# Attention with a top-2 expert layer: a joined prologue, a fourth help tile on VectorE, moved jobs and a last store in two pieces

## The chip, the cores and the metric

One core of one Trainium2 chip runs the whole kernel. The time is that of one execution on the device, in microseconds. Its engines each run their own queue of instructions and meet at semaphores: TensorE (PE) for matmuls and transposes, ScalarE (ACT) for exponentials and copies, VectorE (DVE) for elementwise work, GpSimd (POOL) for indirect transfers and some elementwise work, SyncE (SP) for most transfers.

## What is computed

```python
x: (4, 1024, 128) fp32
xn = layernorm(x)
# attention, 16 heads of 8 channels, rotary positions, on xn
attn = softmax((rope(xn @ Wq.T) . rope(xn @ Wk.T)) * 8**-0.5) . (xn @ Wv.T)
# expert layer on xn: 8 experts, the best 2 of each token, three linear layers
gates = softmax(xn @ gate_w + gate_b); top 2
h = gelu(xn @ w1 + b1); h = gelu(h @ w2 + b2); e = h @ w3 + b3
out = x + attn + sum(top2_gate * e)
```

## The kernel before

**Steps.** Attention is cut into 16 steps (`STEPS`), one for each batch and group of four heads. A step has two halves of 512 queries, and a half has eight blocks (`MT`) of 128 keys: 64 pieces of 128 keys x 512 queries for one head each. For a piece TensorE multiplies keys and queries (the scores, in PSUM), ScalarE takes the exponential into `probs`, and TensorE multiplies it with the values into `o_ps` ("values", one block of four heads at a time). A column of ones in the values gives the sum of the exponentials. After a step VectorE copies `o_ps` (`copy_o`), TensorE transposes the copy (`turn`), and VectorE divides (`normalise`).

**Prologue (L613 to L660, L762 to L858, L1273 to L1320).** The rows of the first batch are normalised (`statistics`, `invert_first`), turned eight in a row with filler matmuls between (L1284, L1287), and projected by `first_projection(g)` (L1300): g = 0 keys and 1 queries of the first 512 rows, 2 and 3 of the second. VectorE multiplies the products with cosine and sine tables (L820, L822); GpSimd or VectorE adds them (L534, L827); ScalarE or GpSimd makes a rounded high part, and the low part is the difference (L541, L829). The parts go from SBUF to `k_st` and `q_st` by transfers (L383, L657) and to DRAM (`store_parts`) for the steps to come. `WARM` (10) and `WARM_AGAIN` (4) filler matmuls run at the start and ahead of the first scores. The scores wait for `k00_loaded` (128 keys), `q0_loaded` and `proj_read` 4.

**Steps 0 and 1** take two heads at a time (1024 columns, L672). **Steps 2 to 8** take three at a time (L694): a half has 11 groups, ten of three heads and the last of two. PSUM holds two groups. The order on TensorE is written out in `step()`: in slot g come the scores of group g + 1, which wait for the exponential of group g - 1; an extra job where `JOB_PLACE` has one (slots 1, 5, 9, 12, 16, 20); and the values of the block that ended in group g - 1. Slots 0, 2, 3, 4, 6, 7, 8 and 10 of a half have values, slots 1, 5 and 9 have none. `plan_jobs()` gives each job its place in sixteenths of a step: `turn` of the step before, `plain` (a projection of a later batch: one matmul of 512 columns, L1343, then `plain_part`, an exchange of rows by SP, and `join_parts` some places later), `values`, `norm`, `count`, `bound`. `ROUTE` spreads the routing arithmetic on VectorE, and `ROUTE_EXP` places its one exponential in ScalarE's queue (L682). All jobs use the one PSUM bank `aux_ps`, and each waits for VectorE's reading of the one before. SP reloads `k_st` and `q_st` half by half; a load for step t waits for the stores of that batch (`stored_before`).

**Experts** (296 to 424 us) run on sorted tokens; the change leaves them alone.

**Steps 9 to 15** (`late_step`) have 20 groups of three (`LATE_ITEMS`): both halves but the first key block of the second half. That block is the help block: four tiles of 128 x 512, whose scores TensorE puts into `aux_ps` one by one in slots 2 to 5 (L1534). VectorE reads the first three (L1192) and makes their exponentials by a polynomial in eight instructions on 128 x 1536 (L1202 to L1210); ScalarE takes the fourth after its eighth group (L733). In slot 17 TensorE waits for both and multiplies them with the values (`help_values`, L1556). Between VectorE's reads stand the additions of expert outputs (`combine`, L1176, six instructions each time), whose rows GpSimd gathers (L610) into the one buffer `gath`. The last step divides its halves apart: `copy_o`, `turn`, `normalise`, `finish_rows` (L1186) and the last store (L502) follow each other.

```python
if HELP_AT <= g < HELP_AT + HG:
    help_scores(t, g - HELP_AT)      # slots 2 to 5
if g == HELP_AT + 7 and not first:
    turn(t - 1, 0, True)             # slot 9
if g == HELP_VALUES:
    help_values(t)                   # slot 17
```

Of the kernel before, what the change touches and what calls it, by code (L numbers as in the profile page):

```python
# [16 lines left out]
F32 = mybir.dt.float32  # L17
# [10 lines left out]
HG = 4  # L28
# [34 lines left out]
WARM = 10  # L63
WARM_AGAIN = 4
WARM_LATE = (3, 1)
FIRST_SCATTER = 66

# [13 lines left out]
def heads_of(g):  # L81

    r = g % HALF_GROUPS
    return [divmod(n, HG) for n in range(3 * r, min(3 * r + 3, MT * HG))]
# [15 lines left out]
LATE_ITEMS = [(0, mt, h) for mt in range(MT) for h in range(HG)] + [(1, mt, h) for mt in range(1, MT) for h in range(HG)]  # L100
LATE_GROUPS = len(LATE_ITEMS) // 3
LATE_BLOCKS = [(0, mt) for mt in range(MT)] + [(1, mt) for mt in range(1, MT)]
HELP_AT = 2
HELP_HEADS = (0, 3, 2, 1)
HELP_VALUES = 17
EXP_COEFFS = (-7.287735462188721, 41.80864715576172, -180.93753051757812, 522.0867309570312, -753.2122192382812)
# [24 lines left out]
TURN_PLACES = (1, MT // 2)  # L131
# [9 lines left out]
def plan_jobs():  # L141

    turns = {BLOCKS * t + TURN_PLACES[t >= GROUPED]: ("turn", t - 1) for t in range(1, SPLIT)}
    fixed = {0: ("values", 0, 2), 7: ("norm", 0), 64: ("norm", 1), 94: ("norm", 2), 126: ("norm", 3), 54: ("count",),
# [8 lines left out]
    for b, places in ((1, (10, 11, 12, 13, 14, 15)), (2, (18, 20, 21, 22, 24, 26)), (3, (27, 28, 30, 31, 32, 34))):  # L153
# [15 lines left out]
ROUTE_EXP = (2, 11)  # L169
ROUTE = {divmod(block, BLOCKS): n for n, block in enumerate((39, 42, 43, 44, 47, 49, 51, 52, 53, 54, 55, 56, 57, 58, 59, 60, 61, 62, 63, 65, 66))}  # L170
# [18 lines left out]
def build(nc, x, Wq, Wk, Wv, w1, b1, w2, b2, w3, b3, gw, gb, rope_cos, rope_sin, consts, out):  # L189
    ctx = ExitStack()  # L190
    with ctx:
# [99 lines left out]
        gath = part(0, 2 * GATHER * C).rearrange("p (k c) -> p k c", c=C)  # L291
        he_s, he_t, he_g, he_p = (part(2 * GATHER * C + 3 * HALF * k, 3 * HALF) for k in range(4))
# [9 lines left out]
        proj_ps = [bank(2, 2), bank(4, 2)]  # L302
# [14 lines left out]
        help_probs = probs[:, PROB_RING - 1]  # L317

        def group_probs(phase, g):
# [7 lines left out]
        names = """x_loaded0 x_loaded0b x_loaded1 x_loaded2 x_loaded3 small_loaded gate_loaded rope_loaded0 rope_loaded1 bias_loaded  # L327
            wT_made wT_copied stats_made std_made rows_made batch_rows_made trans_done xnT0_made proj_done proj_read
            rot_made0 rot_made1 hi_made0 hi_made1 again_made0 again_made1 lo_made0 lo_made1 sq_made0 sq_made1 parts_stored0 parts_stored1 parts_stored2 parts_stored3
            exchanged0 exchanged1 parts_cleared k00_loaded v0_done v0_copied v0_read aux_done aux_read dve_chain dve_pro_chain  # L330
# [5 lines left out]
            gathered combined comb_chain out_ready out_stored  # L336
            fb_loaded fb_v_loaded fb_scores fb_max fb_shift fb_exp fb_turned fb_copied fb_pv fb_chain fb_normed fb_ready fb_stored""".split()
        S = {n: sem(n) for n in names}
        parts_stored, rot_made, hi_made, again_made, lo_made, sq_made, y_stored, xs_in, rope_loaded, exchanged = (
            [S[f"{n}{k}"] for k in range(4 if n in ("parts_stored", "xs_in") else 2)] for n in ("parts_stored", "rot_made", "hi_made", "again_made", "lo_made", "sq_made", "y_stored",  # L340
                                                       "xs_in", "rope_loaded", "exchanged"))
# [5 lines left out]
        def _(sp):  # L347
# [44 lines left out]
            first_load(0, S["k00_loaded"], 0, P)  # L392
            first_load(0, S["ka_loaded"], P, HALF)
# [106 lines left out]
            for n, (tile, tiles) in enumerate([(b * BT, BT) for b in range(B - 1)] + [((B - 1) * BT, BT // 2), (TILES - BT // 2, BT // 2)]):  # L500
# [19 lines left out]
        def _(pool):  # L520
# [83 lines left out]
            for i in range(STEPS - SPLIT - 1):  # L604
                if i >= 1:
                    pool.wait_ge(S["combined"], i)
# [1103 lines left out]
```

## Time and profile before

| | |
|---|---|
| median of 3 runs | 628.67 us (628.52 to 629.24) |
| the profiled execution | 628.49 us, its span 626.7 us |
| busy share of the span | PE 95%, ACT 86%, DVE 54%, POOL 31% |
| chain that ended last | PE 62%, ACT 17%, issue 12%, DVE 5%, DMA 2% |

Times in the rows are microseconds from the start of the span. A matmul's end is modelled, so TensorE's pace is read from start to start. ScalarE's and VectorE's instructions overlap the start of the next a little, and a timeline row joins instructions of one line that follow without a break.

### The profile page before, as it was taken

Reading aid. Unit: us, or ns where it says so; the run is one execution under the profiler, and the core shown is the slowest. Engines: PE = TensorE matmul, PEld = TensorE weight load, DVE = VectorE, ACT = ScalarE, POOL = GpSimd, SP = SyncE. Lnnn points to the kernel's source line nnn. Section 1 sums busy time; section 2 is a strip of 40 time slices with the busy share of each in tenths; the row PEclk is TensorE's granted clock in tenths of the full one; section 3 lists DMA queues with packets and bytes.
Section 4 is the critical chain, followed back from the end, with each engine's and each line's share of the span. In section 5 each row is a group of like instructions: output and inputs, shape, how many; then the busy total and the mean of one; then the engine's idle time right before and its main releaser. Section 6 shows DMA issues by size and latency. Waiting matters only on the chain.

```text
span 626.7 us, 12150 instructions
## 1 busy us (share of the span) xinstructions
PE 595.1 (95%) x4128; PEld 255.9 (41%) x4128; DVE 335.7 (54%) x795; ACT 536.0 (86%) x548; POOL 196.6 (31%) x187
## 2 busy tenths in 40 slices
PE   8889999999999999999999999998999999999996
PEld 6323332232222222232899999983222222222221
DVE  5654322776263335021565555546394958668475
ACT  3799999999999999999455555559999999999995
POOL 2700000000444544441122222223655748484000
PEclk9999999999999999999999999999999999999998
DMA  7653711443264626693433333310312112131311
GB/s 231 171 197 133 264 44 35 162 159 119 85 223 164 219 85 227 205 296 76 99 75 81 71 73 75 75 44 19 110 35 84 59 59 67 55 87 55 116 40 38
DMA packets 82622, 70.69 MB, mean 113 GB/s; under 512 B 44288, under 2 KB 58400, under 8 KB 82576
## 3 DMA queue, kind: packets, MB, share of 16 engines
q1 hardware_dynamic: 76000, 56.34, 29.7%
q0 software_dynamic: 5856, 13.05, 6.8%
q10 hardware_dynamic: 720, 0.71, 0.5%
q8 instruction: 25, 0.41, 0.3%
q14 instruction: 21, 0.17, 0.1%
HBM read 32.92 MB, written 32.96 MB: 105 GB/s over the span
## 4 chain that ended last, share of the span: by engine, by line
PE 62%; ACT 17%; issue 12%; DVE 5%; DMA 2%; ACTq 0%; SPq 0%; DVEq 0%
PE ps L1491 11%; PE ps L1425 10%; ACT probs L729 9%; PE ps L1475 7%; PE ps L1548 6%; ACT probs L694 5%; PE ps L1417 5%; PE ps L1438 5%; PE ps L1521 4%; PE ps L1398 4%; ACT probs L672 2%; PE ps L1343 2%; PE ps L1378 2%; PE ps L1306 1%; DVE x_all L1176 1%
## 5 line engine op out<-in xcount | busy, mean ns | idle before, releaser
L694 ACT ACTIVATE probs<-ps 128x1536 f32<-128x1536 f32 (+1 forms) x154 | 205.2, 1435 | 3.3 <-PE ps L1475 2.9
L729 ACT ACTIVATE probs<-ps 128x1536 f32<-128x1536 f32 x140 | 190.2, 1516 | 2.1 <-PE ps L1521 1.9
L572 POOL DMA_INDIRECT slots_x_d<-xn_all,slot_i x64 | 63.4, 991 | 191.7 <-DVE expert_i L1033 125.0
L1491 PE MATMUL ps<-probs,v_st 128*32 128x512 f32 x896 | 119.3, 605 | 0.6 <-ACT probs L694 0.6
L708 ACT ACTIVATE work<-ps,work 128x256 f32<-128x256 f32 (+1 forms) x156 | 64.9, 455 | 60.4 <-PE ps L1425 60.2
L1548 PE MATMUL ps<-probs,v_st 128*32 128x512 f32 x840 | 111.4, 604 | 0.5 <-DVE o_sb L918 0.5
L610 POOL DMA_INDIRECT work<-slots_y_d,slot_i x64 | 89.8, 1404 | 64.7 <-PE ps L1548 48.5
L1475 PE MATMUL ps<-q_st,k_st 32*128 32x512 f32 x448 | 77.2, 494 | 6.2 <-ACT probs L694 4.5
L1521 PE MATMUL ps<-q_st,k_st 32*128 32x512 f32 x420 | 71.1, 494 | 8.8 <-ACT probs L729 8.7
L1475 PEld LDWEIGHTS ps<-q_st,k_st 32*128 32x128 f32 x448 | 28.9, 181 | 118.9 <-ACT probs L694 91.0
L1521 PEld LDWEIGHTS ps<-q_st,k_st 32*128 32x128 f32 x420 | 26.4, 181 | 108.0 <-ACT probs L729 99.0
L1425 PE MATMUL ps<-work 128*128 128x256 f32 (+1 forms) x312 | 67.9, 361 | 0.0
L672 ACT ACTIVATE probs<-ps 128x1024 f32<-128x1024 f32 x64 | 60.6, 1034 | 3.8 <-PE ps L1378 2.9
L591 POOL DMA_DIRECT2D slots_y_d<-work x39 | 26.7, 685 | 113.3 <-DVE work L1094 108.8
L1425 PEld LDWEIGHTS ps<-work 128*128 128x128 f32 x312 | 53.0, 191 | 5.0
L1208 DVE SCALAR_TENSOR_TENSOR work<-work 128x1536 f32<-128x1536 f32 x28 | 49.2, 1757 | 0.9
L1438 PE MATMUL ps<-work 128*128 128x128 f32 x284 | 38.2, 275 | 0.0
L1438 PEld LDWEIGHTS ps<-work 128*128 128x128 f32 x284 | 37.2, 191 | 1.8 <-issue 0.2
L918 DVE COPY o_sb<-ps 128x512 f32<-128x512 f32 x17 | 11.8, 691 | 47.9 <-PE ps L1548 29.7
L1417 PE MATMUL ps<-work 128*128 128x256 f32 (+1 forms) x156 | 37.2, 361 | 0.0
L1398 PE MATMUL ps<-probs,v_st 128*32 128x512 f32 x256 | 34.1, 604 | 3.0 <-ACT probs L672 2.1
L837 DVE COPY v_st<-v_all 128x128 f32<-128x128 f32 x32 | 8.3, 260 | 41.4 <-PE ps L1491 21.5
(193 smaller groups left out, 552.8 us busy)
## 6 DMA issues: line engine op xcount, KB each, us to landing
k_d<-parts SPq DMA_DIRECT2D x8, 1024.0 KB, 4.6
q_d<-parts SPq DMA_DIRECT2D x8, 1024.0 KB, 5.2
q_st<-q_d SPq DMA_DIRECT2D x30, 256.0 KB, 3.4
k_st<-k_d SPq DMA_DIRECT2D x30, 256.0 KB, 3.0
slots_x_d<-parts SPq DMA_DIRECT2D x5, 1024.0 KB, 7.5
work<-slots_x_d SPq DMA_DIRECT2D x128, 32.0 KB, 1.9
slots_y_d<-work POOLq DMA_DIRECT2D x32, 128.0 KB, 2.2
work<-work SPq DMA_DIRECT2D x24, 128.0 KB, 2.0
```

Of the source, the lines that this page charges most:

```text
L610: nc.gpsimd.indirect_dma_start(out=gath[:, GATHER * c + k, :], out_offset=None, in_=slots_y_d, in_offset=bass.IndirectOffsetOnAxis(ap=slot ...
L672: nc.scalar.activation(probs[:, j % PROB_RING, 2 * pair:2 * pair + 2, :], score_slot(j, pair).rearrange("p (h n) -> p h n", h=2), ACT.Exp, ...
L694: nc.scalar.activation(group_probs(phase, g)[:, 0:size, :], group_slot(g)[:, 0:size * HALF].rearrange("p (h n) -> p h n", n=HALF), ACT.Exp ...
L708: nc.scalar.activation(dst[:, par, k, rows], src[k][:, rows], ACT.Gelu, bias=b12_st[:, par, n, k:k + 1])\
L729: nc.scalar.activation(late_probs(g), group_slot(g).rearrange("p (h n) -> p h n", n=HALF), ACT.Exp, scale=SCALE).then_inc(S["exp_done"], 1)
L1417: nc.tensor.matmul(h1_ps[m][:, 0:units * ST], w1_sb[:, n % 2, m * P:(m + 1) * P], xsT[:, n % 2, 0:units * ST], start=True, stop=True).then ...
L1425: ins = nc.tensor.matmul(h2_ps[m][:, 0:units * ST], w2_sb[:, n % 2, k, m * P:(m + 1) * P], h1[:, n % 2, k, 0:units * ST], start=(k == 0), ...
L1438: ins = nc.tensor.matmul(y_ps[par][:, m, 0:C], h2[:, par, k, m * P:(m + 1) * P], w3_sb[:, par, k, :], start=(k == 0), stop=(k == 1))
L1475: ins = nc.tensor.matmul(group_slot(g)[:, n * HALF:(n + 1) * HALF], k_st[32 * h:32 * h + ROWS, mt * P:(mt + 1) * P], q_st[32 * h:32 * h + ...
L1491: ins = nc.tensor.matmul(o_ps[32 * h:32 * h + 32, :], v_window(mt, h, half), group_probs(phase, half * HALF_GROUPS + g)[:, n, :], start=(j ...
L1521: ins = nc.tensor.matmul(group_slot(g)[:, n * HALF:(n + 1) * HALF], k_st[32 * h:32 * h + ROWS, mt * P:(mt + 1) * P], q_st[32 * h:32 * h + ...
L1548: ins = nc.tensor.matmul(o_ps[32 * h:32 * h + 32, :], v_window(mt, h, half), late_probs(g)[:, k, :], start=begins, stop=ends)
```

## The change

*Prologue.* Identity and weights get their own transfer count (`weights_loaded`); `WARM` is 7, two fillers follow the weights' transposes, the fillers between the row transposes and `WARM_AGAIN` go. The variance is made with fewer small operations (the root takes a scale of 0.25). The order is: first four rows turned, queries projected (g = 1), the first 256 keys' products, the other rows turned, the other keys, g = 2, one value tile group, g = 3. The first 256 keys are rotated, split and loaded apart (`k00_*`). VectorE takes one copy of values and the high parts of g = 2. The first scores wait for `proj_read` 3; block 1's scores are issued ahead of the wait for the value reads.

*Steps 2 to 8.* `first_of` makes the tenth group of a half the one of two heads (27, 28), and the eleventh has three (29, 30, 31); in the last half of step 8 it stays as before. Jobs get new places: `turn` goes to place 6 (slot 9), in step 2 to place 14; `plain` jobs move to places 0, 8 and 12; each join is four or more blocks after its job; the routing pieces follow; the routing exponential goes ahead of group 14 instead of 11. SP waits for the query store only ahead of the query load.

*Steps 9 to 14.* The help block is the first key block of the first half, and VectorE takes all four tiles: its instructions are 128 x 2048 wide. ScalarE has no help exponential. `combine` comes after `normalise`; `gath` has two buffers. In step 15 the help is as before (three tiles and one), and its combine comes after the polynomial.

*End.* The last half is copied in two pieces and turned two tiles at a time, its early columns are summed and stored ahead, and the last sum and store have 32 of the 128 columns.

```diff
-WARM = 10
-WARM_AGAIN = 4
+WARM = 7
+WARM_ROWS = 2
+START_KEYS = 2 * P
+def first_of(r, ending=False):
+    return min(3 * r - (r == HALF_GROUPS - 1 and not ending), MT * HG)
-    return [divmod(n, HG) for n in range(3 * r, min(3 * r + 3, MT * HG))]
+    return [divmod(n, HG) for n in range(first_of(r, ending), first_of(r + 1, ending))]
+LATE_BLOCKS = [(0, mt) for mt in range(1, MT)] + [(1, mt) for mt in range(MT)]
-TURN_PLACES = (1, MT // 2)
+TURN_PLACES = {1: 1, 2: 14}
-    turns = {BLOCKS * t + TURN_PLACES[t >= GROUPED]: ("turn", t - 1) for t in range(1, SPLIT)}
-    fixed = {0: ("values", 0, 2), 7: ("norm", 0), 64: ("norm", 1), 94: ("norm", 2), 126: ("norm", 3), 54: ("count",),
+    turns = {BLOCKS * t + TURN_PLACES.get(t, 6): ("turn", t - 1) for t in range(1, SPLIT)}
+    fixed = {0: ("values", 0, 2), 7: ("norm", 0), 60: ("norm", 1), 92: ("norm", 2), 120: ("norm", 3), 52: ("count",),
-    for g, (made, joined) in enumerate(((40, 43), (44, 48), (46, 50), (56, 60), (70, 74), (76, 80), (78, 82), (86, 90),
-                                        (92, 96), (102, 106), (108, 112), (112, 116)), 4):
+    for g, (made, joined) in enumerate(((36, 40), (40, 44), (44, 48), (48, 52), (64, 68), (72, 76), (76, 80), (80, 84),
+                                        (88, 92), (96, 100), (104, 108), (108, 112)), 4):
-ROUTE_EXP = (2, 11)
+ROUTE_EXP = (2, 14)
...
-                        stored_before(t, 2, 3)
+                        stored_before(t, 2)
                         load_half(k_st, k_d, t, 1, S["kb_loaded"])
+                        stored_before(t, 3)
...
-                    if g == HELP_AT + 5:
+                    if last and g == HELP_AT + 5:
                         nc.scalar.activation(help_probs[:, 0, :], aux_ps, ACT.Exp, scale=SCALE)
...
             for t in range(SPLIT, STEPS - 1):
-                read_help(t)
+                read_help(t, HG)
-                help_exps(t)
+                help_exps(t, HG)
                 if t > SPLIT:
                     normalise(t - 1)
+                    combine(t - SPLIT - 1)
...
-            copy_o(last, 1)
-            normalise(last, (1,))
-            finish_rows((B - 1) * BT + BT // 2, BT // 2).then_inc(S["out_ready"], 1)
+            finish_early_columns().then_inc(S["out_ready"], 1)
+            tail_copy()
+            tail_finish()
...
+            turn_first_rows(0)
             pe.wait_ge(S["wT_copied"], 1)
-            for g in range(4):
-                first_projection(g)
+            first_projection(1, 1)
+            project_start_keys(0)
+            turn_first_rows(1)
+            project_start_keys(1)
+            first_projection(2, 3)
-            for n in range(2):
-                project_values(0, n, v0_ps[n]).then_inc(S["v0_done"], 1)
+            project_values(0, 0, v0_ps[0]).then_inc(S["v0_done"], 1)
+            first_projection(3, 4)
...
-            pe.wait_ge(S["proj_read"], 4)
+            pe.wait_ge(S["proj_read"], 3)
             scores(0, 0, first=True)
+            project_values(0, 1, v0_ps[1]).then_inc(S["v0_done"], 1)
+            pe.wait_ge(S["proj_read"], 4)
```

## Rows read from the trace of the kernel before

**Rows 1.** Table of stretches: busy us (instructions) per engine, clock, DMA share, GB/s
```profile
0.00:24.37 24.37, 22.20 (x88) 14.09 (x88) 13.34 (x43) 9.71 (x23) 10.93 (x14) 1.00 0.62 170
...
86.75:296.40 209.65, 202.85 (x1441) 56.10 (x1441) 86.54 (x221) 205.57 (x157) 63.44 (x64) 1.00 0.47 154
...
424.44:592.50 168.06, 158.71 (x1179) 43.52 (x1180) 115.23 (x166) 166.33 (x129) 90.55 (x65) 1.00 0.21 64
```

**Rows 2.** Timeline of ScalarE, steps 2 to 8: start, us, instruction, [idle before]
```profile
102.73 0.42 ACT L682 ACTIVATE rt<-rt 128x256 f32<-128x256 f32 x1 [0.77 <-DVE rt L954]
...
155.52 7.83 ACT L694 ACTIVATE probs<-ps 128x1536 f32<-128x1536 f32 x6 [0.68 <-PE ps L1475]
...
208.46 87.92 ACT L694 ACTIVATE probs<-ps 128x1536 f32<-128x1536 f32 x66 [0.35 <-PE ps L1475]
```

**Rows 3.** Timeline of TensorE in step 4: scores, values, a projection
```profile
158.84 0.50 PE L1475 MATMUL ps<-q_st,k_st 32*128 32x512 f32 x3
159.28 1.07 PE L1491 MATMUL ps<-probs,v_st 128*32 128x512 f32 x8
...
162.12 1.13 PE L1343 MATMUL ps<-work,wT 128*128 128x512 f32 x2
```

**Rows 4.** Timeline of ScalarE in steps 10 and 11
```profile
462.97 0.60 ACT L733 ACTIVATE probs<-ps 128x512 f32<-128x512 f32 x1
463.44 24.35 ACT L729 ACTIVATE probs<-ps 128x1536 f32<-128x1536 f32 x18
488.12 2.79 ACT L729 ACTIVATE probs<-ps 128x1536 f32<-128x1536 f32 x2 [0.32 <-PE ps L1521]
```

**Rows 5.** Timeline of the prologue, all engines
```profile
9.16 2.14 DVE L804 TENSOR_SCALAR xn_all<-x_all,std 128x128 f32<-128x128 f32 x8
...
11.90 7.08 PE L1300 MATMUL ps<-work,wT 128*128 128x512 f32 x16
...
17.71 0.99 DVE L829 TENSOR_TENSOR parts<-work,parts 128x512 fp32r<-128x512 f32 x1 [0.70 <-ACT parts L646]
...
18.80 0.70 ACTq L657 DMA_DIRECT2D q_st<-parts  x1
...
20.21 3.60 PE L1587 MATMUL ps<-work,zeros 128*128 128x512 f32 x8
```

**Rows 6.** DMA issues of the first 32 us: count, KB each, us to landing
```profile
k_st<-parts SPq DMA_DIRECT2D x1, 256.0 KB, 4.3
...
k_st<-parts SPq DMA_DIRECT2D x1, 64.0 KB, 2.2
```

**Rows 7.** Groups of instructions by shape, VectorE: count, busy us, mean ns, idle before
```profile
L1208 DVE SCALAR_TENSOR_TENSOR work<-work 128x1536 f32<-128x1536 f32 x28 | 49.2, 1757 | 0.9
...
L1186 DVE TENSOR_TENSOR xn_all<-x_all,attn_all 128x1024 f32<-128x1024 f32 x3 | 3.7, 1225 | 0.1
```

**Rows 8.** Timeline of VectorE in steps 9 and 11
```profile
431.61 0.96 DVE L1202 TENSOR_SCALAR work<-work 128x1536 f32<-128x1536 f32 x1
...
483.14 0.69 DVE L1192 TENSOR_SCALAR work<-ps 128x512 f32<-128x512 f32 x1 [0.49 <-PE ps L1534]
483.75 1.66 DVE L1176 SCALAR_TENSOR_TENSOR x_all<-work,gates,x_all 128x128 f32<-128x128 f32 x6
...
488.22 0.96 DVE L1202 TENSOR_SCALAR work<-work 128x1536 f32<-128x1536 f32 x1
...
499.17 1.76 DVE L1210 SCALAR_TENSOR_TENSOR probs<-work 128x1536 f32<-128x1536 f32 x1
```

**Rows 9.** Timeline of TensorE: the help values of steps 9 and 11
```profile
448.59 1.06 PE L1556 MATMUL ps<-probs,v_st 128*32 128x512 f32 x8
...
504.24 1.06 PE L1556 MATMUL ps<-probs,v_st 128*32 128x512 f32 x8
```

**Rows 10.** Timeline of VectorE at the end
```profile
622.19 0.29 DVE L930 TENSOR_TENSOR attn_all<-ps,o_rec 128x128 f32<-128x128 f32 x1
622.51 0.69 DVE L1186 TENSOR_TENSOR xn_all<-x_all,attn_all 128x512 f32<-128x512 f32 x1
```

**Rows 11.** DMA issues of the last 27 us
```profile
out_dram<-xn_all SPq DMA_DIRECT2D x2, 256.0 KB, 2.7
```

More of the change, by code:

```diff
@@ new lines, in turn_start_keys @@
+            def turn_start_keys(piece, table):
+                cols = slice(piece * START_KEYS, (piece + 1) * START_KEYS)
+                done, signal = (("k00_proj", "k00_read"), ("proj_done", "proj_read"))[piece]
+                dve.wait_ge(S[done], (1, 3)[piece] + table)
+                dst, src = (t_cos, t_sin)[table], (cos_sb, sin_sb)[table]
+                ins = nc.vector.tensor_tensor(dst[:, 0, cols], proj_ps[0][:, table * HALF + cols.start:table * HALF + cols.stop], src[:, cols], ALU.mult)
+                if table:
+                    ins.then_inc(S[signal], 1)
@@ new lines, in _, with turn_first_rows @@
+            ins.then_inc(S["wT_made"], 1)
+            for _ in range(WARM_ROWS):
+                nc.tensor.matmul(aux_ps[:, 0:HALF // 2], zeros[:, 0:P], zeros[:], start=True, stop=True)
+            def turn_first_rows(half):
+                for k in range(4 * half, 4 * half + 4):
+                    pe.wait_ge(S["rows_made"], k + 1)
+                    ins = nc.tensor.transpose(bank(half)[:, (k % 4) * C:(k % 4 + 1) * C], xn_all[:, k, :], ident)
+                ins.then_inc(S["trans_done"], 1)
@@ L1301, in first_projection, with project_start_keys @@
                                      start=True, stop=True).then_inc(S["proj_done"], 1)
+            def project_start_keys(piece):
+                lo, hi = piece * START_KEYS, (piece + 1) * START_KEYS
+                if piece:
+                    pe.wait_ge(S["k00_read"], 1)
+                for s in range(2):
+                    nc.tensor.matmul(proj_ps[0][:, s * HALF + lo:s * HALF + hi], weights(0, s), xnT[:, 0, lo:hi],
+                                     start=True, stop=True).then_inc(S[("k00_proj", "proj_done")[piece]], 1)
@@ L1400, in values, with turn @@
                 ins.then_inc(S["pv_done"], 1)
-            def turn(t, half=0, helped=False):
-                if helped:
-                    pe.wait_ge(S["help_exp"], t - (SPLIT - 2))
+            def turn(t, half=0, helped=None):
+                if helped == "late":
+                    pe.wait_ge(S["help_read"], (t - (SPLIT - 2)) * HG)
+                elif helped == "last":
+                    pe.wait_ge(S["help_exp"], 1)
                 free_aux(aux_of_turn(t, half))
@@ L1517, in late_scores @@
                     pe.wait_ge(S["kb_loaded"], t * 16 + 16)
+                if not last and (1, 0, 0) in items:
+                    pe.wait_ge(S["q1_loaded"], t * 16 + 16)
                 if g >= 2 or not first:
@@ L1562, in late_step @@
                     if g < LATE_GROUPS - 1:
-                        late_scores(t, g + 1, first=(first and g == 0))
+                        late_scores(t, g + 1, first=(first and g == 0), last=last)
                     elif not last:
@@ L1571, in late_step @@
                     if HELP_AT <= g < HELP_AT + HG:
-                        help_scores(t, g - HELP_AT)
-                    if g == HELP_AT + 7 and not first:
-                        turn(t - 1, 0, True)
+                        help_scores(t, g - HELP_AT, last)
+                    if g == 9 and not first:
+                        turn(t - 1, 0, "last" if last else "late")
                     if g == 13 and last:
@@ L1577, in late_step @@
                     if g == HELP_VALUES:
[L1578 removed]
+                        help_values(t, last)
                     if g > 0:
@@ L1584, in late_step @@
                         late_values(t - 1, len(LATE_BLOCKS) - 1)
-            for _ in range(WARM_AGAIN):
-                nc.tensor.matmul(bank(0), zeros[:, 0:P], xnT[:, 0, 0:HALF], start=True, stop=True)
+            pe.wait_ge(S["proj_read"], 3)
+            scores(0, 0, first=True)
+            project_values(0, 1, v0_ps[1]).then_inc(S["v0_done"], 1)
             pe.wait_ge(S["proj_read"], 4)
-            scores(0, 0, first=True)
             for t in range(GROUPED):
```

350 lines of the change are left out of this document (210 added, 140 removed).

## The prediction

> **What bounds the kernel now.** I read the table of stretches first. From the first exponential at 24.37 the work is attention; two long stretches of it and the expert part in between hold most of the span. In steps 2 to 8 ScalarE is busy for 205.57 of 209.65 us and TensorE for 202.85; in steps 9 to 14 166.33 and 158.71 of 168.06 [rows 1]. So both engines are near full, and what a cut is worth depends on which has slack at that place. The timeline of ScalarE comes next: the reader is to see how few breaks there are. In steps 2 to 8 it waits 0.77 us for the routing table and 0.68 at the fourth step's second half of keys; steps 6 to 8 run 66 exponentials in 87.92 us, 29.3 a step, after a break of 0.35 [rows 2]. A three-head exponential follows its predecessor after 1.33 us (18 in 24.35 [rows 4]), a two-head one is followed after about 0.90. On TensorE a group's three score matmuls take 0.43 us of its time and a block's eight value records 1.0, so a slot with both lasts 1.43: 0.10 more than the exponential beside it; a slot without values has 0.9 to spare, and a projection of 1.06 uses it [rows 3]. In steps 9 to 14 the step lasts 27.85 us (from 463.44 to 491.28 in that pattern: 18 exponentials, a break of 0.31 to 0.32, two more, the help exponential) [rows 4].
>
> **Term 1, the prologue.** What is removed: on VectorE's chain the scaling by a half, one add and the shift (five small operations, of which three are replaced by two that lie beside ScalarE's root and then cost 0.1), at 0.20 each: the rows are normalised from about 8.2 instead of 9.16. The filler matmuls between the transposes go, and the first half's rows are projected before the second half is turned. Four rows of eight in 2.14 us [rows 5] put the copy at about 9.6 and the first projection at 10.3 instead of 11.90: -1.6. The queries' projection (four records, 1.7 us) now comes first and the keys' start (two matmuls of half width, 0.9) behind it, where before each of the pair took 1.7 and the query parts were ready only at 18.80 [rows 5]. Counted through (products on VectorE 0.7 each, two, the sum 0.7, the rounding copy on ScalarE 0.6, the low part 0.7 to 1.0), the query parts are ready at 15.2 and the start keys' at 16.1. A load of 256 KB took 4.3, one of 64 KB 2.2 [rows 6]; I take 3.7 for the queries (near the 4.3, but nothing large beside it) and 0.7 behind them for 128 KB of keys: 19.6. TensorE, which has two more projections and one value job in its queue, is free at 19.7. The scores can start there instead of when the last filler ends (20.21 + 3.60 = 23.8 [rows 5]): -4.0. Given back: the value tiles of the first batch are now read after the last products, so the second block's values wait for VectorE until 22.7 (about 0.6), and the second half of keys is ready at 23.85, half a microsecond later than now; with 4.3 it lands at 28.1 where block 4 would want it at 27.8 (0.4). **-3.0**; bounds -4.0 (nothing given back) and -0.5 (both loads as slow as with the stores beside them).
>
> **Term 2, steps 2 to 8.** The root cause of the routing wait goes, since that exponential is asked for three groups later (its own 0.3 stays): -0.7. The key load waited for a store of group 7, which is now joined eight blocks earlier; the load of keys no longer waits for the query store either: -0.7 [rows 2]. The two-head group: before, its 0.90 lay beside a slot with values (1.43) and a further one (1.43) followed; TensorE lost 0.53 + 0.10 against a slack of 0.47 (two exponentials, 2.66, less an exponential's 1.45 and 0.7 for signal and scores), so ScalarE stopped for up to 0.35 at a half's start. Now it lies beside slot 9, which never has values. But three value slots (0.30 behind, less 0.14 for the smaller group) come just ahead, and in every step the turn of 0.6 is put into that very slot: 0.43 + 0.6 against 0.90. Kept slot by slot through the seven steps with the new places of the jobs, this gains 0.6 in all, since TensorE's own sum of a half (32 heads at 0.143, 8 blocks at 1.0, one to two jobs) is within 0.6 us of ScalarE's 14.3 either way. **-2.0**; bounds 0 (the moved jobs cost what the waits gave) and -4.5 (a stop of 0.35 gone at each of 13 halves more).
>
> **Term 3, steps 9 to 14.** ScalarE loses the help exponential (463.44 - 462.97 = 0.47) and the break of 0.31, which with its ripple is 0.46: 0.93 less up to slot 17 [rows 4]. VectorE gets a fourth tile. Widths: 1024 columns took 1225 ns, 1536 took 1757, so 2048 take 2290; single-source ones go from 0.96 to 1.23 us (a third wider, less the fixed part) [rows 7, 8]. Six of the one and two of the other: +3.7, a chain of 16.4 instead of 12.7 (488.22 to 500.93). The first read was at 483.14 and comes 0.17 earlier, as it no longer waits for the second half of queries; four reads follow each other at 1.43, no combine (1.66 each) between them: the chain starts at 488.0 and ends at 504.45 [rows 8]. The help values ran at 504.24 [rows 9], and would now run at 503.3. TensorE stands still in front of them until 504.55, with the last scores of the step queued behind. So those start 0.3 later than before, and as TensorE sets the pace from there, the step is 0.3 *longer*: 28.15. In step 9 there was no combine and no break: the chain started at 431.61 and would start at 432.87 for the fourth read; it ends at 449.3 against 448.59 [rows 8, 9]: +0.8. The combine (3.3) moves behind the normalising, in front of the copy of the sums; that copy is wanted 5.3 after the chain's end, and 0.9 + 3.3 + 0.3 (and 1.2 in steps 11 to 13) lie ahead of it: covered, just. 0.8 + 5 x 0.3 = **+2.3**; bounds -4.8 (no wait at all) and +7.
>
> **Term 4, the end.** Copy and turn in halves: the first two transposes run beside the second copy, -0.25. The last sum is 128 elements wide instead of 512: 0.29 instead of 0.69 [rows 10]. The store is 64 KB instead of 256: 2.7 was the median [rows 11], 2.2 took 64 KB elsewhere [rows 6]: -0.4. The page "DMA: Bandwidth & Descriptors" of the Trainium skill (Specifications) says that pieces under 512 B fall below line rate; these have 128 B, and by it this last 0.4 would not come. No row here has such pieces going to memory. **-1.1**, bounds -1.4 and -0.6. Buffers for two gathers and the later flag count cost nothing: the gathers are a whole step ahead of their combine.
>
> **Sum.** -3.0 - 2.0 + 2.3 - 1.1 = -3.8. The profiled execution took 628.49 us (span 626.7): 624.7. The median of the runs is 0.18 higher: **624.9 us**. About 0.2% (1.3 us) is what a measurement here can tell from no change.
>
> **The rivals.**
> *The help chain is hidden after all* (the width costs less, or TensorE is later than I think): then a late step falls to 27.0, and term 3 is -4.8: 617.8 us. For it: 3.3 us of slack before. Against: 3.7 longer and 0.93 sooner wanted. 0.12.
> *The two-head group is worth the whole stop* at each half: term 2 is -4.5, 622.4. 0.12.
> *TensorE's clock falls in the prologue.* It was granted in full throughout [rows 1], with fillers in every gap; now there are some two us with only four transposes and then nothing ahead of the projections. At the lower level (1.2 GHz) the 1.7 us of the query projection and the rest in line become 1.8 longer: term 1 is -1.2, 626.7. The page "TensorE: Matmul & The Clock Gate" (Parts 1 and 4) says that an idle stretch puts the clock back to half and that transposes do not count as busy. 0.10.
> *The key loads come late* beside the stores: term 1 is -1.0, 626.9. 0.08.
> *Slower: VectorE becomes the bound of the late steps.* Its loop has reads 5.0, chain 16.4, normalise 0.9, combine 3.3, finish 1.2, two value copies 0.4 and the copy of the sums 0.7: 27.9 of 28.15. The other terms give 6.1, so it decides from 28.9 a step on; if its waits make 29.2 of it, term 3 is 0.8 + 5 x 1.35 = 7.6 and the time 630.2. For it: combine stands in front of the copy that TensorE waits for. Against: the overlaps of back-to-back copies (0.08 each). 0.08.
> My forecast has the remaining 0.50, with 623.0 to 626.8 as its own range.
>
> **The numbers.** Leaving out the hidden chain and the slow loop (0.20) gives 620.0 to 627.3. Faster by over 0.2% (below 627.4): the forecast, the first four rivals nearly whole: 0.85. Within 0.2%: the upper edges, 0.08. Slower: 0.07.
>
> **What would show it.** First exponential near 20.4, the ninth near 28.9; no wait for the routing table or a key load in steps 2 to 4; steps 2 to 8 in 207.6; in steps 10 to 14 a wait of TensorE's help values for VectorE of about 1.2 us and a step of 28.1 to 28.2. A late step under 27.5, or no such wait, would prove term 3 wrong; score matmuls 0.85 apart ahead of 13 us, the clock; a copy of the sums that starts over 0.3 after its last value matmul, the slow rival.

## The result, and the profile after

The changed kernel takes 631.33 us (median of 20 runs, 628.73 to 633.59 but for one of 1793) against 628.48 for the kernel before: a ratio of 1.0041, 95% interval 1.003 to 1.0052. I had forecast 624.9 in a range of 620.0 to 627.3, so it went the other way, by 6.4 us from the forecast. The profiled execution took 630.17 us, with a span of 628.4 us where the kernel before had 626.7. It is one of the changed kernel's shorter ones, which matters below.

The table of stretches of the changed kernel, cut at the same events as [rows 1], but for the last row's end: here it is the start of step 15 (592.83), there it lay 1.6 us inside that step:

```profile
0.00:22.11 22.11, 18.02 (x61) 11.12 (x62) 13.23 (x40) 8.12 (x22) 7.27 (x13) 1.00 0.70 186
85.61:295.87 210.26, 201.92 (x1441) 56.06 (x1441) 86.84 (x221) 204.99 (x156) 62.86 (x64) 1.00 0.47 153
423.93:592.83 168.90, 152.93 (x1168) 41.24 (x1169) 141.54 (x167) 163.25 (x121) 113.56 (x65) 1.00 0.21 61
```

The first exponential comes 2.3 us earlier. Steps 2 to 8 take 210.26 instead of 209.65, with less busy time on both engines than before: there is more waiting. Step 15 began at 590.92 before; from 424.44 that made 166.48, now it is 168.90. The gain of the first row is gone by then.

The timeline of ScalarE in steps 2 to 8 of the changed kernel (it answers [rows 2]):

```profile
105.15 0.44 ACT L727 ACTIVATE rt<-rt 128x256 f32<-128x256 f32 x1
...
115.33 11.11 ACT L739 ACTIVATE probs<-ps 128x1536 f32<-128x1536 f32 x8 [0.41 <-PE ps L1614]
128.30 3.87 ACT L739 ACTIVATE probs<-ps 128x1536 f32<-128x1536 f32 x3 [1.86 <-PE ps L1614]
132.59 14.46 ACT L739 ACTIVATE probs<-ps 128x1536 f32<-128x1536 f32 x11 [0.42 <-PE ps L1614]
147.32 29.42 ACT L739 ACTIVATE probs<-ps 128x1536 f32<-128x1536 f32 x22 [0.27 <-PE ps L1614]
177.15 29.37 ACT L739 ACTIVATE probs<-ps 128x1536 f32<-128x1536 f32 x22 [0.40 <-PE ps L1614]
```

The wait for the routing table (0.77) and the one for keys (0.68) are gone. In their place stands one that the kernel before did not have, 1.86 us at 128.30. TensorE's timeline names it:

```profile
124.44 0.50 PE L1614 MATMUL ps<-q_st,k_st 32*128 32x512 f32 x3
126.72 0.67 PE L1478 MATMUL ps<-rt,cst 128*128 128x256 f32 x2 [1.78 <-DVE rt L1061]
```

L1478 is the count of the routed rows, L1061 makes the masks that it multiplies. The change asks for the count at block 52 instead of 54, and the masks are not ready. VectorE is not idle; it is full, as its timeline shows (start, us; the rows left out follow without a gap as well):

```profile
122.77 0.69 DVE L993 TENSOR_TENSOR parts<-work,parts 128x512 fp32r<-128x512 f32 x1
123.38 0.42 DVE L994 CAST parts<-parts 128x512 fp32r<-128x512 f32 x1
123.72 0.42 DVE L1055 TENSOR_TENSOR rt<-rt,gates 128x256 f32<-128x256 f32 x1
...
126.15 0.43 DVE L1061 TENSOR_TENSOR rt<-rt 128x256 f32<-128x256 f32 x1
```

In the kernel before, the masks (L978) and the count (L1350) stood so, on VectorE and TensorE:

```profile
130.52 0.42 DVE L978 TENSOR_TENSOR rt<-rt 128x256 f32<-128x256 f32 x1
131.25 0.70 PE L1350 MATMUL ps<-rt,cst 128*128 128x256 f32 x2
```

The masks were done 0.3 us ahead of the count. The change makes them 4.4 us earlier (126.58 instead of 130.94), but has TensorE ready for the count 6.3 us earlier (124.94 instead of 131.25). The 0.3 could be read ahead of the result.

Step 3 takes 32.0 us for that, after 29.62 before. In steps 10 to 14 (28.1 to 28.2 each, 27.8 to 27.9 before) the reader is to see the break of ScalarE, TensorE's wait in front of the help values, and the chain of VectorE that it waits for:

```profile
478.70 27.31 ACT L774 ACTIVATE probs<-ps 128x1536 f32<-128x1536 f32 x20 [0.88 <-PE ps L1662]
```

```profile
505.33 1.07 PE L1700 MATMUL ps<-probs,v_st 128*32 128x512 f32 x8 [1.20 <-DVE probs L1319]
```

```profile
488.83 1.23 DVE L1311 TENSOR_SCALAR probs<-work 128x2048 f32<-128x2048 f32 x1
490.10 2.29 DVE L1313 SCALAR_TENSOR_TENSOR work<-probs,work 128x2048 f32<-128x2048 f32 x1
...
502.99 2.29 DVE L1319 SCALAR_TENSOR_TENSOR probs<-probs,work 128x2048 f32<-128x2048 f32 x1
...
509.53 1.23 DVE L1270 TENSOR_TENSOR xn_all<-x_all,attn_all 128x1024 f32<-128x1024 f32 x1
...
510.81 0.68 DVE L1001 COPY o_sb<-ps 128x512 f32<-128x512 f32 x1
```

At the end (answering [rows 10]) VectorE's last sum is 0.29 wide instead of 0.69, and the DMA issues of the last 29 us (answering [rows 11]) say what the store made of it:

```profile
624.21 0.29 DVE L1294 TENSOR_TENSOR xn_all<-x_all,attn_all 128x128 f32<-128x128 f32 x1
```

```profile
out_dram<-xn_all SPq DMA_DIRECT2D x1, 256.0 KB, 2.6
out_dram<-xn_all SPq DMA_DIRECT2D x1, 192.0 KB, 2.8
out_dram<-xn_all SPq DMA_DIRECT2D x1, 64.0 KB, 3.3
```

So the profiled executions account for themselves: -1.14 up to the start of step 2 (86.75 to 85.61), +0.63 from there to step 9 (337.69 to 338.32; the expert part in it is unchanged), +2.42 in steps 9 to 14, -0.22 from there on; together +1.7. The medians differ by 2.85. The other 1.16 is not in this execution: it had the full clock until its last 0.6 us, and of the 19 runs only four had a mean granted clock of 0.997 or more (628.7 to 630.2 us, 629.5 in the mean). The other fifteen had 0.990 to 0.995 and took 630.4 to 633.6. Of the 68 runs of the kernel before that were taken beside the experiments, 57 had 0.997 or more. (At 0.997 nothing need be lost: the profiled execution of the kernel before has it, and its clock falls at 623.54, behind TensorE's last transposes.)

### The profile page after: what moved, and what is told of

Read it like the earlier page. It is cut to its first block, busy times and chain, and to the rows that moved or that the text cites. A ratio compares the mean times of both kernels' runs of the same rounds, so it can differ in the third digit from the quotient of the medians.

```text
span 628.4 us, 12073 instructions
## 1 busy us (share of the span) xinstructions
PE 586.8 (93%) x4106; PEld 251.5 (40%) x4106; DVE 366.6 (58%) x805; ACT 532.5 (85%) x541; POOL 218.4 (35%) x188
## 4 chain that ended last, share of the span: by engine, by line
PE 57%; DVE 21%; ACT 10%; issue 7%; DMA 2%; POOL 1%; ACTq 0%; SPq 0%; DVEq 0%; POOLq 0%
PE ps L1630 11%; PE ps L1564 10%; DVE probs L1317 10%; ACT probs L739 7%; PE ps L1614 7%; PE ps L1691 6%; PE ps L1556 5%; PE ps L1577 5%; PE ps L1662 3%; PE ps L1526 3%; DVE probs L1319 2%; DVE work L1313 2%; ACT probs L774 2%; PE ps L1471 1%; PE ps L1506 1%
## 5 line engine op out<-in xcount | busy, mean ns | idle before, releaser
L658 POOL DMA_INDIRECT work<-slots_y_d,slot_i x64 | 112.8, 1763 | 45.8 <-PE ps L1691 29.6
L639 POOL DMA_DIRECT2D slots_y_d<-work x39 | 26.8, 687 | 113.5 <-DVE work L1177 109.0
L1317 DVE SCALAR_TENSOR_TENSOR probs<-probs,work 128x2048 f32<-128x2048 f32 (+1 forms) x21 | 46.5, 2215 | 0.7
L1301 DVE TENSOR_SCALAR work<-ps 128x512 f32<-128x512 f32 x27 | 18.7, 692 | 20.4 <-PE ps L1677 20.4
```

The lines of the kernel that those rows point to most:

```text
L658: nc.gpsimd.indirect_dma_start(out=gath[:, i % 2, GATHER * c + k, :], out_offset=None, in_=slots_y_d, in_offset=bass.IndirectOffsetOnAxis( ...
L1317: ins = nc.vector.scalar_tensor_tensor(power, rest if k == 3 else power, EXP_COEFFS[k - 3], rest, ALU.add, ALU.mult)
```

## The experiments

All start from the changed kernel. Each had 4 to 12 runs beside the kernel before, whose median stayed at 628.36 to 628.44.

**1. Fillers again in the prologue.**

```diff
-WARM_ROWS = 2
+WARM_ROWS = 4
@@ turn_first_rows(half)
+                    if k % 4 < 3 and half == 0:
+                        nc.tensor.matmul(aux_ps[:, 0:C // 2], zeros[:, 0:P], zeros[:, 0:C // 2], start=True, stop=True)
+                for _ in range(3 - half):
+                    nc.tensor.matmul(aux_ps[:, 0:HALF // 2], zeros[:, 0:P], zeros[:], start=True, stop=True)
```

> The changed kernel with fillers in the prologue again: two more ahead of the first rows, one between each two of the first four transposes, three behind them and two behind the second four. The profiled execution of the changed kernel had the full clock throughout, and its 630.17 lies near the lower end of the runs (median 631.33), most of which show a mean granted clock of 0.992 to 0.995. Theory (TensorE's clock falls in the prologue in most executions, where it now stands still three times for 0.5 to 0.8 us): with the fillers the mean clock of the runs is 0.999 or 1.0 again and the median comes to 629.0 to 629.6; the stretch to the first exponential stays at 22.1. Rival (it falls somewhere else, in the late steps where TensorE waits for the help tiles, or at the end): the clocks stay at 0.992 to 0.995 and the median at 631.0 to 631.6. Second rival (the fillers cost as much as they keep): clock 1.0, and the first exponential 0.5 later or more.

Measured: 632.4 us (1.0047, 1.0031 to 1.0064; 0.8 above even the rival's range), and a clock under 0.997 in five of seven runs. The fillers do not bring the median down: the first rival holds in that the clock falls elsewhere, though not in the late steps, which it named first. The profiled execution, this time one of the long ones, shows where. TensorE's timeline and the table of stretches:

```profile
124.31 0.50 PE L1618 MATMUL ps<-q_st,k_st 32*128 32x512 f32 x3
126.61 1.19 PE L1482 MATMUL ps<-rt,cst 128*128 128x256 f32 x2 [1.79 <-DVE rt L1061]
...
129.31 1.94 PE L1634 MATMUL ps<-probs,v_st 128*32 128x512 f32 x8
...
133.94 1.07 PE L1634 MATMUL ps<-probs,v_st 128*32 128x512 f32 x8
```

```profile
126.36:133.18 6.82, 6.57 (x26) 2.16 (x26) 4.02 (x13) 2.60 (x2) 0.00 (x0) 0.50 0.23 86
```

The clock falls to its lower level (1.2 GHz) within TensorE's wait for the masks, and stays there for 6.8 us: eight value records last 1.94 instead of 1.07, and step 3 takes 35.0 us instead of 32.0.

**2. The count job later.**

```diff
-120: ("norm", 3), 52: ("count",),
+120: ("norm", 3), 56: ("count",),
-... 49, 50, 51, 53, 54, 55, 56, 57, 58, 59, 60, 61, 62, 63, 64))}
+... 49, 50, 51, 56, 57, 58, 59, 60, 61, 62, 63, 64, 65, 66, 67))}
```

> The changed kernel with the count job four blocks later (block 56 instead of 52, two places on in its step) and the twelve routing stages behind it three blocks later. In the changed kernel TensorE waits 1.78 us for the masks in front of the count, and step 3 takes 32.0 us instead of 29.62. Theory (the count was asked for before VectorE had made the masks; nothing else is late there): step 3 takes 30.1 to 30.3, the sum of steps 2 to 8 is 208.4 to 208.6 instead of 210.3, and the run is 1.8 us shorter, 629.5. Rival (VectorE has more work in steps 2 and 3 than their time holds, so the wait turns up at the next job that it serves, a turned block or a projected part): steps 2 to 8 stay at 209.8 to 210.3 and the run at 630.8 to 631.3.

Measured: 627.07 us, 0.9979 (0.9967 to 0.999), 4.3 less than the changed kernel and below the kernel before; 8 of 12 runs with 0.997 or more. Step 3 takes 29.94, and from step 2 to step 9 it is 336.2 instead of 338.3. So 2.1 us are in the profile and nothing else was late; the median gains twice that. ScalarE's timeline has no break inside step 3 any more. This row begins one exponential ahead of the step, with a break that the changed kernel has as well (0.41 at 115.33):

```profile
116.70 29.52 ACT L739 ACTIVATE probs<-ps 128x1536 f32<-128x1536 f32 x22 [0.41 <-PE ps L1614]
```

**3. The wait filled, the count left early.** Zero matmuls in front of the wait, first eight, then four:

```diff
                 free_aux(AUX[("count",)])
+                for _ in range(8):
+                    nc.tensor.matmul(aux_ps[:, 0:HALF // 2], zeros[:, 0:P], zeros[:], start=True, stop=True)
                 pe.wait_ge(S["masks_made"], 1)
```

> The changed kernel with eight zero matmuls of 256 columns (0.21 us each) on TensorE ahead of its wait for the masks; the count job stays at its early place, so the stop of ScalarE stays. In the profiled executions of two variants TensorE's granted clock fell to 0.5 at the start of this wait (126.4 and 126.8) for 6.8 us, and step 3 took 35.0 us instead of 32.0. Theory (the wait costs twice: 1.8 us of itself, and 3.0 in the executions in which the clock falls in it): with TensorE at work in the wait step 3 takes 31.9 to 32.3, the mean clock of the runs is 0.997 or more in most of them, and the median is 628.7 to 629.4. Rival (the clock falls at that place whatever TensorE does in the 1.8 us, for it follows from the work before): step 3 at 35.0 in most runs, clocks of 0.992 to 0.995 and a median of 631.0 to 631.6.

Measured: 630.63 us (1.0034, 1.0021 to 1.0046), five of seven runs at 0.998. The eight were too many (3.72 us), step 3 took 33.6, and still the median was not above the changed kernel's (the intervals overlap). With four:

> As the run with the filled wait, with four zero matmuls instead of eight: there the eight took 3.72 us (0.45 each in place of the 0.21 that I had reckoned), so that TensorE came 1.5 us late out of them and step 3 took 33.6. Four take 1.8 and end with the wait. Theory (the wait costs 1.8 us of itself, and 3.0 more in the executions in which the clock falls in it): step 3 at 31.9 to 32.2, mean clock of most runs 0.997 or more, median 628.9 to 629.4, which is two less than the changed kernel. Rival (the clock is not what parts 631.3 from 629.1): median 630.8 to 631.4 whatever the clocks say.

Measured: 629.38 us (1.0012, 0.9999 to 1.0025); ten of eleven runs with 0.997 or more. Step 3 takes 31.9, and TensorE's and ScalarE's timelines show that the stop is still there:

```profile
124.26 1.99 PE L1477 MATMUL ps<-zeros 128*128 128x256 f32 x8
126.09 0.62 PE L1480 MATMUL ps<-rt,cst 128*128 128x256 f32 x2
```

```profile
127.62 3.88 ACT L739 ACTIVATE probs<-ps 128x1536 f32<-128x1536 f32 x3 [1.79 <-PE ps L1616]
```

This parts the two prices. With TensorE at work in the same stop the median is 1.95 lower: that is the clock. It fits the four runs of the changed kernel with the full clock, whose mean of 629.5 is as low. The 2.1 of step 3 is the wait itself.

**4. The help values two groups later.**

```diff
-HELP_VALUES = 17
+HELP_VALUES = 19
```

> The changed kernel with the four value matmuls of the help tiles two groups later (behind group 19's scores instead of group 17's, still ahead of the step's last block). Late steps take 28.1 to 28.2 now. Theory A (the only price of the fourth tile is TensorE's wait of about 1.3 us in front of these matmuls): without that wait all of steps 10 to 14 fall to 27.0 to 27.3, 5 us less in all, 626.3. Theory B (VectorE's own loop of 27.9 us is right behind it): the steps in which VectorE also finishes a batch (11 to 13) stay at 27.9 to 28.0 and only 10 and 14 fall to 27.0 to 27.4, 2.0 to 2.5 us in all, 629. Theory C (the order of the combine behind the normalising holds the copy of the sums): steps stay at 28.1 or grow.

Measured: 627.31 us (0.9984, 0.9971 to 0.9998). Steps 10 to 14 take 27.45, 27.43, 27.73, 27.96, 27.96, and step 9 takes 26.6: between theories A and B (in this execution the clock fell in step 3 again, which took 35.0). TensorE no longer waits for the chain, VectorE's loop does become the bound, but only after two steps have used up its slack. A third thing bounds before it: a break of 0.36 at each step's start, where the help values, two blocks' values and two groups' scores follow each other on TensorE.

**5. Three tiles on VectorE, the fourth on ScalarE.** (In all late steps what the last one does.)

```diff
-                    if last and g == HELP_AT + 5:
+                    if g == HELP_AT + 5:
@@ the loop over the late steps
-                read_help(t, HG)
+                read_help(t, HG - 1)
-                help_exps(t, HG)
+                help_exps(t, HG - 1)
```

> The changed kernel with only three help tiles of 512 columns on VectorE and the fourth as an exponential of ScalarE behind group 7 in steps 9 to 14, as its last step has it; the first half's tile, the places and the combine behind the normalising stay. Theory (the fourth tile, 3.7 us of chain, is what makes the late steps longer): the steps take 27.8 to 27.9 as in the kernel before, TensorE's help values wait for nothing, and the run is 2.4 us shorter, 628.9. Rival (moving the combine behind the normalising, in front of the copy of the sums, is what costs): the steps stay at 28.0 to 28.2. Second rival (three tiles in the new order are better than the order before): 27.5 or less, 627.3.

Measured: 625.23 us (0.9938, 0.9925 to 0.9951). The late steps take 27.4, which is the second rival: less than the 27.85 of the kernel before. ScalarE's timeline has no break left:

```profile
462.41 0.66 ACT L778 ACTIVATE probs<-ps 128x512 f32<-128x512 f32 x1
462.88 27.08 ACT L774 ACTIVATE probs<-ps 128x1536 f32<-128x1536 f32 x20
489.80 0.66 ACT L778 ACTIVATE probs<-ps 128x512 f32<-128x512 f32 x1
```

From step 9 to step 15 it is 164.10, against 168.90 in the changed kernel and 166.48 before. So the fourth tile costs 4.8 us there, and what else the change does to these steps gains 2.4 (the first half's tile, which waits for no second load, or the combine out of the gaps between the reads: no run parts the two). The median fell by 6.1, more than 4.8. None of its six runs had a clock of 0.994 or less, which may be the rest; experiment 6 compares without the wait in step 3.

**6. Both (2 and 5).**

> Both changes that gained by themselves: the count job at block 56 and three help tiles. Theory (they lie in different stretches and add up): late steps of 27.4, steps 2 to 8 in 208.5, and 627.07 less six times 0.7 to 0.8, so 622.4 to 623.2. Rival (a part of the gain of three tiles over 631.33, 6.1 us where its late steps give 4.3, came from the clock holding in step 3 in its few runs): then the same 622.4 to 623.2 here; if the gain of the three tiles is really 6.1, the median is 621.0.

Measured: 622.1 us (0.9903, 0.9887 to 0.9919), all four runs at 0.997 or more. It is 5.0 below experiment 2, where the late steps give 4.8, so the parts add up, and it beats both kernels.

**7. The constants in one load.** Edit: the identity is no longer loaded ahead of the weights; `consts` is loaded whole behind them.

> The count job at block 56, and in the prologue the constants in one load behind the three weights, as in the kernel before, instead of the identity alone ahead of them. The rows of the first batch landed at 5.31 and 6.38 in the changed kernel where the kernel before had 4.38 and 5.40, so the first normalised row came no earlier although the chain in front of it is shorter. Theory (the identity's load ahead pushes the rows' transfers back): rows land near 4.4 and 5.4, the first projection starts at 10.5 to 10.8 instead of 11.5, the first exponential at 21.1 to 21.4 and the median is 626.2 to 626.5. Rival (that second was this execution's own, or comes from elsewhere): rows at 5.0 to 5.4 and 6.1 to 6.4 or the same projection start, and 627.0. Second rival (the weights come later without the identity ahead and TensorE waits for them): the weights' transposes later than 8.0, 627.3 or more.

Measured: 627.23 us (0.9984, 0.9975 to 0.9993): nothing. VectorE's and TensorE's timelines:

```profile
4.49 1.86 DVE L812 BATCH_NORM_STATS2 stats<-x_all 128x6 f32<-128x128 f32 x8 [4.34 <-DMA x_all<-in_L_attn_x_dram]
```

```profile
7.62 0.55 PE L1389 MATMUL ps<-cst,w_raw 128*128 128x128 f32 x3 [0.72 <-DMA cst<-in_consts_dram]
```

The rows land at 4.5 here and at 4.5 to 4.9 in the eleven other executions of these variants, with the identity's own load: the 5.31 of the changed kernel's profile was its own, and the theory fell.

**8. The old groups.**

```diff
-    return min(3 * r - (r == HALF_GROUPS - 1 and not ending), MT * HG)
+    return min(3 * r, MT * HG)
```

> The count job at block 56, and the two-head group again the last of each half in all of steps 2 to 8. Theory (my term: the new place of that group is worth 0.6 us in all): 627.7, steps 2 to 8 in 209.1. Rival (it is worth the whole stop of 0.35 at each half's start): 4.5 us, 631. Rival (nothing, or the other way: the new place puts the small group beside the turn, and a stop of 0.40 stands at each step's start): 626.3 to 627.2, steps 2 to 8 in 208.0 to 208.5 or less.

Measured: 628.65 us (0.9998, 0.9986 to 1.0011), with only 4 of 11 runs at 0.998 or more (627.2 to 627.5). From step 2 to step 9 it is 336.9 instead of 336.2: the new place is worth 0.65, as I had kept it slot by slot. ScalarE's timeline would mislead here, for it shows not one break from the routing exponential to the end of step 8:

```profile
104.95 189.02 ACT L739 ACTIVATE probs<-ps 128x1536 f32<-128x1536 f32 x140
```

Yet the median distance from one three-head exponential to the next is 1.42 us, where experiment 2 has 1.33: the pauses are shorter than that view lists, and there are many. Why the other seven runs had a mean clock of 0.995 or 0.996 stays open; its profile is not one of them.

**9. Four tiles, with the combine woven in,** and the same with experiment 1's fillers. Edit: HELP_VALUES = 19; `combine` takes a range of its twelve instructions, and `read_help` puts a quarter of the earlier combine ahead of each read; a batch is finished one step later; count at 56.

> The count job at block 56; four help tiles, with the help values behind group 19's scores; and on VectorE the combine cut into four parts of three instructions each, put ahead of each read of a help tile where it waits 0.4 to 0.8 us for TensorE, and the finishing of a batch one step later. Theory (with four tiles ScalarE has only the 20 exponentials of 1.335, if neither TensorE's wait nor VectorE's loop of 27.9 is in the way): late steps of 26.6 to 27.0, so 5 x 0.5 to 0.8 us less than with three tiles, 618.5 to 620.0. Rival (TensorE is the next bound: 20 x 0.43 for scores, 16 x 1.0 for values, 0.6 for the turn and four help tiles): the same 26.6 or less by its sum of 25.6, so it would show only as stops of ScalarE around the turn and the help values; steps of 27.1 to 27.4 and 621 to 622. Second rival (the reads, pushed back by the parts of the combine, make the chain late for group 19): TensorE waits at the help values and steps stay at 27.5 or more, 623 or more.

Measured: 623.7 us (0.9914, 0.9893 to 0.9935). Steps 10 to 14 take 27.4, the first rival: ScalarE stops for 0.37 at each step's start, as in experiment 4, behind this on TensorE:

```profile
504.61 1.07 PE L1705 MATMUL ps<-probs,v_st 128*32 128x512 f32 x8
505.50 1.04 PE L1696 MATMUL ps<-probs,v_st 128*32 128x512 f32 x8
506.47 0.50 PE L1667 MATMUL ps<-q_st,k_st 32*128 32x512 f32 x3
506.90 1.06 PE L1696 MATMUL ps<-probs,v_st 128*32 128x512 f32 x8
```

Slot 17 is one that has no block's values of its own; slot 19 has, and so has the one behind it. At slot 17 the chain of four is not ready, at slot 19 the values don't fit: four tiles come out level with three. The last step is 0.6 longer on top (27.4 us from its first to its last exponential, 26.8 in experiment 6).

> The same with the prologue's fillers. Theory (they hold TensorE's clock in the prologue, where it fell in some executions at 11.8 and at 23.8 to 25.4 us, for 3.4 us each, and made the ninth exponential 2.6 us late in one): fewer runs with a mean clock of 0.995 to 0.996, a median 0.3 to 0.8 below the run without them. Rival (the fall at 24 us is not reached by fillers that end at 15): the same share of such runs and the same median within 0.3.

Measured: 623.15 us (0.9906, 0.9887 to 0.9925), all five runs at 0.997 or more, where four of six were without fillers. With so few runs that is a hint only. What a fall in the prologue costs can be read, though. The execution without fillers had two low stretches of 3.4 us, at 12.0 and at 25.7, and its ninth exponential came at 32.45; with fillers and a full clock it came at 30.05, the first exponential being level (22.05 and 21.98). So the second stretch cost 2.4 us by then, of which 1.4 were left at the start of step 2. An earlier one, at 11.3 in experiment 10's execution, made the queries' projection last 3.56 us instead of 1.96, and the first exponential came at 23.3. A row of the table of stretches from experiment 2's execution, which had two as well:

```profile
25.45:28.85 3.40, 3.40 (x19) 0.73 (x21) 3.37 (x13) 0.45 (x2) 3.25 (x4) 0.50 0.41 52
```

**10. One whole store at the end,** 256 KB in rows of 512 bytes in place of 192 KB and 64 KB.

> The count job at block 56, and at the end one store of 256 KB with whole rows of 512 bytes instead of 192 KB early and 64 KB in pieces of 128 bytes last. The 64 KB took 2.6 to 3.4 us from issue to landing in nine profiled executions, the 256 KB ahead of them 2.4 to 2.7. Theory (pieces of 128 bytes take as long as four times the bytes in whole rows, or longer): landing in 2.6 to 2.7, median 0 to 0.5 below 627.07. Rival (my term: fewer bytes land 0.4 sooner): 627.4 to 627.6.

Measured: 627.26 us (0.9976, 0.9964 to 0.9989), level with experiment 2. The stores took

```profile
out_dram<-xn_all SPq DMA_DIRECT2D x2, 256.0 KB, 2.9
```

which is the middle of 2.7 and, for the last one, 3.1; the 64 KB in pieces of 128 bytes took 2.6 to 3.4 in twelve executions (3.0 in the mean). A quarter of the bytes brings nothing that the median shows.

## Why the prediction was wrong

- **Term 2, steps 2 to 8, is the step that failed most, and turned the sign.** I counted -2.0; it was +0.6. What I had named came nearly as I wrote it: with the count out of the way (experiment 2) the stretch is 1.45 shorter than before, 0.65 of it by the grouping. But under "kept slot by slot ... with the new places of the jobs" I kept TensorE's time alone. I did not ask, for each job moved earlier, when VectorE would have its operand ready. The joins and routing stages were moved earlier too, into a VectorE without idle time around 123 us, and the count, which had 0.3 us to spare, two blocks up: +2.08 (experiment 2).
- **The clock.** My rival had the mechanism and a chance of 0.10 but the wrong place: it fell in the wait that I had missed. Experiment 3 takes 1.95 us off the median by keeping TensorE at work in it. The page "TensorE: Matmul & The Clock Gate" of the Trainium skill (Part 1) says that an idle stretch puts the clock back to half. The traces agree in part: of four profiled executions with this wait of 1.8 us unfilled the clock fell in two, and in neither of the two with it filled. In the prologue, where I had put it, it fell in some executions as well (at 11.3 to 12.0 or 23.8 to 25.7 us), in neither of the two profiled ones with fillers there. The profiled run of the changed kernel shows none of this.
- **Term 1, the prologue,** came out at half: -1.14 in the profile, -1.5 as the mean start of step 2 (85.24) in six executions of this prologue without a fall of the clock, where I had -3.0. In such an execution (experiment 6's) normalising began at 8.48 (8.2 forecast), the first projection at 10.76 (10.3), and the query parts were ready at 16.2 (15.2): the low part took 1.26 us beside an addition of GpSimd, where I had 0.7 to 1.0. The first exponential came at 21.5 (20.4). What is given back until step 2 was 0.6 to 1.6 in the six executions, where I had 1.0. VectorE's timeline of that execution, and below it GpSimd's:

```profile
14.93 1.26 DVE L885 TENSOR_TENSOR parts<-work,parts 128x512 fp32r<-128x512 f32 x1
```

```profile
14.92 0.72 POOL L595 TENSOR_TENSOR work<-work 128x256 f32<-128x256 f32 x1 [11.00 <-DVE work L872]
```

- **Term 3, the late steps,** was right in size (+2.3 forecast, +2.42 measured), in its step (28.15; 28.1 to 28.2) and in its mechanism (a wait of 1.2 us in front of the help values). Experiment 5's step of 27.4 is the 27.85 of before less the 0.46 that I had counted for the break. The rival of the hidden chain is out. That of VectorE's loop was close by: it is 0.2 to 0.3 behind, as experiment 4 shows.
- **Term 4, the end,** brought 0.22 instead of 1.1. VectorE's side gave 0.6 or so; the store's 0.4 did not come, and 0.4 more was lost (3.9 us from the last sum's end to the span's end, 3.5 before). The 2.7 of [rows 11] was the wrong price too, being the middle of two stores (2.3 and 3.0); the last one alone took 3.0, as the row below shows, and the 64 KB of the changed kernel 3.3. The page "DMA: Bandwidth & Descriptors" of the Trainium skill (Specifications), which I had set beside the term, was the better guide: it puts pieces under 512 bytes below line rate, and the twelve executions agree, with 3.0 in the mean for a quarter of the bytes. The DMA issues of the last 4 us before:

```profile
out_dram<-xn_all SPq DMA_DIRECT2D x1, 256.0 KB, 3.0
```

- **The sum.** Of -3.0 - 2.0 + 2.3 - 1.1 the first, second and last term were too hopeful by 1.9, 2.6 and 0.9 in the profile, and the third by 0.1: 5.5 from -3.8 to +1.7. The clock adds 1.2 in the median over this execution, and 1.9 over the mean of the four runs with the full clock.
- **The range** left out a slower side of its own for term 2. The term's upper bound of 0 was no bound: a job whose place is moved ahead of its operand can cost any time up to what its producer lacks.
- **Readings that were off without deciding it.** The 168.06 us that I took for steps 9 to 14 [rows 1] hold 1.6 us of step 15; no term used them. The bound of -4.5 in term 2 counts thirteen stops of 0.35 alone; with the two waits it would be -5.9, some 621 us, and [rows 2] has 66 exponentials without such a stop. The slack of 0.47 is 0.51 by its own terms.

## What to carry to other kernels

Where a list of places for jobs is changed, every job needs two readings: what it takes on the engine that runs it, and when the engine that feeds it will be done, above all in the stretch in which the feeding engine has no idle time. Here the wait on TensorE cost itself (2.1 us) and, in many runs, a stretch at half its clock (3.0 more); look at the granted clock of all runs before you take the profiled one for the typical one. And work moved off the bounding engine is paid where it is waited for: the fourth tile freed 0.5 us of ScalarE a step and cost TensorE 1.2.

## What the runs showed of the hardware that I had not expected

- The granted clock fell within a wait of TensorE of only 1.8 us that lay between two busy stretches (126.4 and 126.8 us), and stayed at 0.50 for 6.8 us, though TensorE was busy for 6.57 of 6.82: 3.0 us on step 3.
- With the same wait the clock falls in some executions and not in others: step 3 took 32.0 in two and 35.0 in two of the four profiled ones, which are four variants with the same work in step 3. The runs of the changed kernel spread over 4.9 us, those of the kernel before over 3.4, eighteen of its twenty over 1.1.
- The subtraction of the query's low part, 512 columns on VectorE, took 1.26 us in eleven executions of the new prologue, with an addition of 256 columns on GpSimd (0.72) that began just before it. In the two in which it began just before GpSimd's (at 15.87 and 15.89 in one) it took 0.69, and GpSimd's 1.25 to 1.27. Whichever began second took 0.5 to 0.6 us longer, most of the other's time.
- Writing 64 KB in pieces of 128 bytes took 2.6 to 3.4 us, 256 KB in rows of 512 bytes 2.3 to 3.1.
